# Attention outputs divided by their row sums, causal scores in row tiles, and the probability copies shared evenly by two engines

## The reference

```python
# block 1: heads are mixed in the scores, and the softmax is normalised over the image
# block 2: causal attention; then a quantized FFN
# block 3: causal attention with biases; then a mixture of four experts, two of them active
p = softmax(mask(q @ k.T * HD ** -0.5))     # 256 x 256 a head
o = p @ v
y = o @ w_proj (+ b_proj)
x = x + y
```

## Time and profile before

| | us |
|---|---|
| median of 3 runs | 978.55 |
| lowest and highest | 974.76 and 978.98 |
| profiled execution, whole | 974.61 |
| profiled execution, span | 972.6 |

### The profile page before, as it was taken

How to read it: one execution, slowest core, us unless ns; L and a number is a source line. 1 busy time by engine, 2 the same in 40 slices (tenths; PEclk the granted TensorE clock), 3 DMA queues, 4 the chain that set the end, 5 groups by cost and what they waited for, 6 DMA issues and landing times.

```text
span 972.6 us, 19124 instructions
## 1 busy us (share of the span) xinstructions
PE 808.0 (83%) x5550; PEld 630.5 (65%) x5550; DVE 772.7 (79%) x2166; ACT 632.9 (65%) x1931; POOL 192.6 (20%) x234
## 2 busy tenths in 40 slices
PE   0876698889988755899999486559999997999997
PEld 0762576667766653678887356438778877677775
DVE  7327799999999835699999869938999994688886
ACT  0211587777877513689888564248889874688885
POOL 9001423443234110000000000010000010134344
PEclk9997899999999967799999798779999995799999
DMA  5000000000000091466666200035666650313130
GB/s 184 1 0 1 1 1 0 0 0 0 0 0 0 10 121 28 76 93 97 90 87 83 31 1 1 0 62 83 84 97 96 88 75 0 69 41 82 41 82 17
DMA packets 54355, 44.30 MB, mean 46 GB/s; under 512 B 28592, under 2 KB 42544, under 8 KB 54192
## 3 DMA queue, kind: packets, MB, share of 16 engines
q1 hardware_dynamic: 53872, 42.30, 27.9%
q0 software_dynamic: 448, 1.57, 0.6%
HBM read 12.33 MB, written 3.21 MB: 16 GB/s over the span
## 4 chain that ended last, share of the span: by engine, by line
PE 44%; DVE 12%; DMA 3%; issue 1%; ACT 1%; SPq 1%; POOL 0%; POOLq 0%; DVEq 0%; ACTq 0%
PE ps L839 7%; PE ps L850 6%; PE ps L720 6%; PE ps L624 6%; PE ps L670 5%; PE ps L661 3%; PE ps L626 3%; DVE chst L910 2%; DMA qk<-lo 2%; DVE on L929 2%; PE ps L551 1%; PE ps L634 1%; PE ps L635 1%; PE ps L647 1%; PE ps L826 1%
## 5 line engine op out<-in xcount | busy, mean ns | idle before, releaser
L419 ACT ACTIVATE ee<-ps,nmax 128x128 f32<-128x128 f32 (+1 forms) x588 | 249.5, 443 | 11.7 <-DVE nmax L990 9.9
L1031 DVE TENSOR_SCALAR ee<-ee,rrec 128x128 f32<-128x128 f32 (+1 forms) x588 | 174.8, 360 | 5.2
L720 PE MATMUL ps<-w,ee 128*128 128x128 f32 x960 | 137.0, 279 | 19.9 <-DVE ee L1031 19.9
L406 ACT ACTIVATE big<-ps 128x384 f32<-128x384 f32 (+1 forms) x224 | 113.5, 538 | 40.0 <-PE ps L720 39.4
L720 PEld LDWEIGHTS ps<-w,ee 128*128 128x128 f32 x960 | 103.9, 141 | 45.4 <-DVE ee L1031 35.6
L419 ACT ACTIVATION_READ_ACCUMULATOR ee<-ps,nmax 128x1 f32 x588 | 124.2, 211 | 0.0
L990 DVE TENSOR_REDUCE nmax<-ps 128x2 f32<-128x256 f32 x200 | 101.1, 545 | 18.0 <-PE ps L626 18.0
L624 PE MATMUL ps<-qk 128*128 128x128 f32 (+1 forms) x400 | 103.7, 348 | 13.4 <-DMA qk<-lo 10.8
L296 POOL TENSOR_TENSOR big<-qs,w 96x256 f32<-96x256 f32 x108 | 78.8, 761 | 144.4 <-ACT qs L429 144.4
L1234 DVE TENSOR_TENSOR hhl<-ee,hhl 128x512 fp32r<-128x512 f32 x96 | 81.7, 858 | 27.9 <-ACT hhl L525 26.2
L624 PEld LDWEIGHTS ps<-qk 128*128 128x128 f32 x400 | 79.8, 207 | 31.7 <-issue 17.9
(11 more groups left out here) (224 smaller groups left out, 1365.5 us busy)
## 6 DMA issues: line engine op xcount, KB each, us to landing
qk<-hi SPq DMA_DIRECT2D x36, 192.0 KB, 3.7
qk<-hi SPq DMA_DIRECT2D x72, 96.0 KB, 3.8
qk<-lo SPq DMA_DIRECT2D x36, 192.0 KB, 4.8
qk<-lo SPq DMA_DIRECT2D x72, 96.0 KB, 4.6
big<-moe_gate SPq DMA_DIRECT2D x8, 768.0 KB, 6.9
w<-w_in SPq DMA_DIRECT2D x1, 1831.5 KB, 12.9
xc<-x_in SPq DMA_DIRECT2D x4, 384.0 KB, 5.7
l_mix<-on SPq DMA_DIRECT2D x8, 192.0 KB, 6.6
```

What stands on the lines that cost most here:

```text
L406: nc.scalar.activation(et[:, h, 0:w], ps[:, 4 + hh, 0:w], ACT.Copy).then_inc(own(l, f"et{hh}"), 1)
L419: last = nc.scalar.activation(ee[:, ke, hh, qc, 0:w], src, ACT.Exp, bias=nmax[:, kp, hh, qc:qc + 1], accum_out=rsum[:, kp, hh, qc:qc + 1])
L720: last = nc.tensor.transpose(ps[:, 4 + hh, b * P:(b + 1) * P], ee[:, u, hh, qc, tc * P:(tc + 1) * P], ident)
L1031: last = V.tensor_scalar(v, v, rrec[:, kp, hh, qc:qc + 1], None, ALU.mult)
```

## The change

- The probabilities are not scaled. The values get a column of ones beside each head's 16 (in the half that was zero), so that the weighing yields the row sums too. `normalise_outputs` divides: the unscaled outputs are transposed so that queries lie on partitions (L665 in the new numbering), VectorE takes the reciprocal of the sums (L1043) and multiplies (L1050). In block 1 that takes the place of a copy. In blocks 2 and 3 the result `ob` is transposed back (`outputs_back`, L672), copied by ScalarE to `oc` (L446) and then projected (`project_outputs`, L679); the projection weights are 96 columns in place of 2 x 96.
- In block 1 the sum of squares comes from bn_stats of the unscaled probabilities, four a unit (each 256 columns), and six small instructions after the loop combine them with the squared reciprocals.
- Causal scores are made in row tiles: `qk` holds two heads in 64 rows each, four groups of 16 rows a head. The two heads' products of one query tile follow each other in different halves of the array; the mask is one product per head over both diagonal blocks, after all four. The 16-row groups of the two heads are filled by 12 DMAs an image with half the rows each.
- ScalarE copies three of the six probability tiles an image, VectorE three; before it was four and two.
- The last block's weight split has a buffer of its own and is made earlier, before block 2's attention.

```diff
-STK = 16 * 6
+STK = 16 * 12
...
-        qk = sb("qk", [P, 2, NH, 2, N], F32R)
+        qk = sb("qk", [P, 2, NH // 2, 2, N], F32R)
...
                         for t, a0, a1 in moves:
-                            sp.dma_start(qk[t * HD:(t + 1) * HD, par, :, a0:a1, :].bitcast(F32),
-                                         part[:, a0:a1, :].bitcast(F32)).then_inc(own(l, "stacked"), 16)
+                            for hh in range(2):
+                                r0 = hh * 4 * HD + t * HD
+                                sp.dma_start(qk[r0:r0 + HD, par, :, a0:a1, :].bitcast(F32),
+                                             part[hh * (C // 2):(hh + 1) * (C // 2), a0:a1, :].bitcast(F32)).then_inc(own(l, "stacked"), 16)
...
-                    last = nc.scalar.activation(ee[:, ke, hh, qc, 0:w], src, ACT.Exp, bias=nmax[:, kp, hh, qc:qc + 1],
-                                                    accum_out=rsum[:, kp, hh, qc:qc + 1])
+                        last = nc.scalar.activation(ee[:, ke, hh, qc, 0:w], src, ACT.Exp, bias=nmax[:, kp, hh, qc:qc + 1])
...
+            def outputs_by_channel(l, i):
+
+                act.wait_ge(*upto(l, "oc_ps", i + 2))
+                nc.scalar.activation(oc[0:C, :], ps[0:C, 6, 0:N], ACT.Copy).then_inc(own(l, "oc"), 1)
...
+                            r0 = hh * 4 * HD
+                            mm(ps[:, 2 * kp + hh, qc * N:qc * N + w], qk[r0:r0 + 4 * HD, par, u, 0, qc * P:(qc + 1) * P],
+                               qk[r0:r0 + 4 * HD, par, u, 1, 0:w], start=(qc == 0), stop=False)
+                    for hh in range(2):
+                        diag = ps[:, 2 * kp + hh, :].rearrange("p (b t) -> p b t", t=P)[:, 0::3, :]
+                        last = mm(diag, identb[:, :], mid_dim(maskb[:, :], 1, TPI), start=False, stop=True)
...
+            def outputs_back(l, i):
+
+                pe.wait_ge(*upto(l, "on", i + 2))
+                for q in range(TPI):
+                    last = nc.tensor.transpose(ps[0:C, 6, q * P:(q + 1) * P], ob[:, q, :], ident)
+                last.then_inc(own(l, "oc_ps"), 1)
+
+            def project_outputs(l, i):
+
+                pe.wait_ge(*upto(l, "oc", i + 2))
+                for q in range(TPI):
+                    last = mm(ps[:, 6, q * C:(q + 1) * C], oc[0:ONE + 1, q * P:(q + 1) * P], wa(f"l{l}_p", ONE + 1), start=True, stop=True)
...
+                        if l > 1 and u == 2:
+                            project_outputs(l, i - 1)
                         for hh in range(2):
-                            pe.wait_ge(*upto(l, "norm", 2 * k + (hh + 1)))
+                            pe.wait_ge(*upto(l, "exp", 2 * k + (hh + 1)))
...
                         if u == 0:
                             project_qk(l, i + 2, par)
+                            if l > 1:
+                                outputs(l, i - 1)
                         if u == 1:
-                            outputs(l, i - 1)
+                            if l == 1:
+                                outputs(l, i - 1)
+                            else:
+                                outputs_back(l, i - 1)
...
+            def normalise_outputs(l, i):
+
+                dve.wait_ge(*upto(l, "oq", i + 2))
...
+                V.reciprocal(rec, src[:, :, :, HD]).then_inc(own(l, "orec"), 1)
+                dve.wait_ge(*upto(l, "orec", i + 2))
+                for q in range(TPI):
...
+                    last = V.tensor_tensor(dst.rearrange("p (h d) -> p h d", d=HD), src[:, q, :, 0:HD], last_dim(rec[:, q, :], HD), ALU.mult)
+                last.then_inc(own(l, "on" if l > 1 else "added"), 1)
```

More of the change, by code:

```diff
@@ L652, in outputs @@
                 pe.wait_ge(*upto(l, "ot", i + 2))
-                if l == 1:
+                for q in range(TPI):
                     for g in range(2):
-                        for q in range(TPI):
-                            a = (q * 2 + g) * C
-                            last = nc.tensor.transpose(ps[:, 6, a:a + C], ots[0:C, g, q * P:(q + 1) * P], wb("ident", C)[:, 0:C])
-                else:
-                    for t in range(TPI):
-                        for g in range(2):
-                            last = mm(ps[:, 6, t * C:(t + 1) * C], ots[:, g, t * P:(t + 1) * P], wa(f"l{l}_p")[:, g * C:(g + 1) * C],
-                                      start=(g == 0), stop=(g == 1))
+                        a = (q * 2 + g) * C
+                        last = nc.tensor.transpose(ps[:, 6, a:a + C], ots[0:C, g, q * P:(q + 1) * P], wb("ident", C)[:, 0:C])
+                last.then_inc(own(l, "oq"), 1)
+            def outputs_back(l, i):
[7 more added lines that the diff above has]
+                    last = mm(ps[:, 6, q * C:(q + 1) * C], oc[0:ONE + 1, q * P:(q + 1) * P], wa(f"l{l}_p", ONE + 1), start=True, stop=True)
                 last.then_inc(own(l, "out_ps"), 1)
@@ L1010, in add_outputs @@
             def add_outputs(l, i):
                 dve.wait_ge(*upto(l, "out_ps", i + 2))
-                if l == 1:
-                    for q in range(TPI):
-                        src = ps[:, 6, q * 2 * C:(q + 1) * 2 * C].rearrange("p (h d) -> p h d", d=2 * HD)[:, :, 0:HD]
-                        dst = on1[:, q, i + 1, :] if isinstance(i, int) else on1[:, q, bass.ds(i + 1, 1), :].rearrange("p a c -> p (a c)")
-                        last = V.tensor_copy(dst.rearrange("p (h d) -> p h d", d=HD), src)
-                else:
-                    tv = tok_all[:, bass.ds(i * TPI + TPI, TPI), :]
-                    last = V.tensor_tensor(tv, ps[:, 6, 0:TPI * C].rearrange("p (t c) -> p t c", c=C), tv, ALU.add)
@@ L1021, in add_outputs @@
-                last.then_inc(own(l, "added"), 1)
-            def normalise(l, k, kp, ke):
-                dve.wait_ge(*upto(l, "exp", 2 * k + 2))
-                V.reciprocal(rrec[:, kp, :, :], rsum[:, kp, :, :]).then_inc(own(l, "rec"), 1)
-                dve.wait_ge(*upto(l, "rec", k + 1))
-                for hh in range(2):
-                    for qc in range(TPI):
-                        v = ee[:, ke, hh, qc, 0:scores_cols(l, qc)]
-                        last = V.tensor_scalar(v, v, rrec[:, kp, hh, qc:qc + 1], None, ALU.mult)
-                    last.then_inc(own(l, "norm"), 1)
+                tv = tok_all[:, bass.ds(i * TPI + TPI, TPI), :]
@@ L1034, in _ @@
+                V.tensor_tensor(tv, ps[:, 6, 0:TPI * C].rearrange("p (t c) -> p t c", c=C), tv, ALU.add).then_inc(own(l, "added"), 1)
             for l in (1, 2, 3):
@@ L1058, in _ @@
                         maxima(l, k + 2, j % 2)
-                        if l > 1 and u != 1:
+                        if l > 1 and u == 2:
+                            add_outputs(l, i - 1)
+                        if l > 1:
                             w = len(blocks(l)) * P
-                            dve.wait_ge(*upto(l, "tr", TR0 + 2 * k + 1))
-                            V.tensor_copy(et[:, 2 * u, 0:w], ps[:, 4, 0:w]).then_inc(own(l, "et0"), 1)
+                            for hh in range(1):
+                                dve.wait_ge(*upto(l, "tr", TR0 + 2 * k + hh + 1))
+                                V.tensor_copy(et[:, 2 * u + hh, 0:w], ps[:, 4 + hh, 0:w]).then_inc(own(l, f"et{hh}"), 1)
@@ L1063, in _ @@
                         if l == 1:
-                            dve.wait_ge(sg("l1_norm"), 2 * k + 2)
-                            dve.wait_ge(sg("l1_ssq"), TR0 + k)
-                            for hh in range(1 if u == 2 else 2):
-                                a = ee[:, u, hh, :, :].rearrange("p q t -> p (q t)")
-                                last = V.tensor_tensor_reduce(out=sqj[:, hh, :], in0=a, in1=a, scale=1.0, scalar=0.0, op0=ALU.mult,
-                                                              op1=ALU.add, accum_out=ssq[:, par, 2 * u + hh:2 * u + hh + 1])
@@ L1070, in _ @@
-                            last.then_inc(sg("l1_ssq"), 1)
+                            dve.wait_ge(sg("l1_exp"), 2 * k + 2)
+                            for hh in range(2):
+                                for q in range(TPI):
+                                    last = V.bn_stats(est[:, par, q, 2 * u + hh, :], ee[:, u, hh, q, :])
+                            last.then_inc(sg("l1_est"), 1)
                             if u == 2:
-                                dve.wait_ge(sg("l1_ssq"), TR0 + k + 1)
-                                dve.wait_ge(sg("l1_ssq_act"), i + 1)
-                                V.tensor_copy(ssqa[:, bass.ds(i, 1), :].rearrange("p a h -> p (a h)"), ssq[:, par, :]).then_inc(sg("l1_ssqa"), 1)
```

115 lines of the change are left out of this document (66 added, 49 removed).

## The result

The changed kernel takes **1055.54 us** (median of 4 runs, 1054.69 to 1061.57), the kernel before 978.0 (4 runs, 974.76 to 978.98): a ratio of 1.081, 95% interval 1.077 to 1.086. It is slower by 8%; the forecast was 1042.

The account below looks back on a forecast made before the run. The causal loops were taken as bound by the longer of the DMA cycle, 11.2 us, and TensorE's turn, 10.5. 75 + 8 + 7 - 26 + 2 = +66 on 974.6 gave 1041, forecast 1042 us; band 1030 to 1050, range 1003 to 1068.

Parts of the forecast that it names:

- Block 1's loop, -26: First block's attention loop: without scaling, transposes wait for the exponentials alone; 1.62 us less an image, 26 us for 16.
- VectorE's cover: First block's loop: VectorE finishes reciprocal and products about 1 us before TensorE's weighing; without that, at most 5 us return.
- Behind block 1, +2: After the first block's loop: about six linked VectorE instructions, at most 0.33 us each, precede the variance; +2 us.
- The stack DMAs, 11.2: Causal loops: six more issues add 3.7 us, a shorter landing returns 1.1; the DMA cycle grows from 8.62 to 11.2 us.
- TensorE's own turn, 8.9, with the wait 10.5: Causal loops: TensorE's work 8.9 us an image, no gain from row tiles; waiting 1.6 for normalised outputs makes 10.5.
- The loops, +75: Both causal loops: +2.5 us an image over 15 periods in each of two layers, +75 us.
- Ahead of and behind the loops, +8 and +7: Around the causal loops: two stacks in series ahead, +8 in all; five hand-overs and the new wait behind, +3.5 each.
- dear tiles: Rival, causal loops: score unit 1.2 us, TensorE's turn 11.4 to 11.9, or idle time lowers the clock; +87, 1062; chance 0.14.
- Cheap issues: Rival, causal loops: a 48-row issue costs about half, so TensorE's turn of 10.5 us holds; +40, 1015 us; chance 0.22.
- Faster: Rival, causal loops: VectorE has outputs ready, TensorE never late at the transposes back; period 8.0, -38, 937 us; chance 0.06.
- the wait for `on`: Causal loops, u=1: TensorE waits 1.6 us for normalised outputs before transposing back; loss and gain cancel at period 9.3.
- The signs named beforehand: Right: block 1's image -1.6, bursts 11 us apart, `ob` wait 1.5 or more. Wrong: issues near 0.3, unit below 0.7, clock below 1.

Follow-up runs that it names:

- one move on VectorE: Changed kernel with VectorE's reciprocal and two output products put ahead of the middle head pair's maxima in blocks 2 and 3: 998.38 us, ratio 1.021.
- the run that filled the wait: Changed kernel with three more unused q-projection products an image on TensorE, ahead of the transposes back in blocks 2 and 3: 1022.57 us, ratio 1.046.
- the repaired whole change: Changed kernel with its output path half a head pair earlier on three engines and three of twelve stacking transfers issued by GpSimd: 985.42 us, ratio 1.008.
- the kernels with GpSimd's transfers: Three of twelve stacking transfers issued by GpSimd: kernel before plus row tiles 980.62 us, also with block 1's change 962.28, changed kernel with earlier output path 985.42.
- the row tiles alone: Kernel before with only the row-tiled scores and twelve stacking transfers in blocks 2 and 3, old sums and scaling kept: 1010.02 us, ratio 1.033.

## Why the prediction was right, and where not

- **Block 1's loop, -26.** Right: an image takes 11.81 us instead of 13.50, 1.69 less where I had 1.62, which is 27 in 16 images, and the one wait was gone. VectorE's cover held, and bn_stats took 0.35 us each (192 of them in 67.0 us of busy time) in the place of 0.33.
- **Behind block 1, +2.** Too small: it was 27 - 23.1 = +3.9 up to the product of the sums of squares. VectorE's linked instructions took from 301.37 to 304.47, 3.1 us, since some have 384 elements and take 0.7; TensorE waited 4.00 us for them, where it had waited 0.71. A consequence that I didn't have at all came behind it: the clock is 0.50 from 305 to 325, and the 32 products that took 3.74 us take 7.03. That is 3.3 of the +4.5 up to block 2.
- **The stack DMAs, 11.2.** The issues were right (0.63 against 0.62). The term that failed is the landing: I took 3.5, the least of the trace of before, for the last transfer of half the bytes; it was 2.08. The cycle is 9.7 to 9.9, **below** TensorE's turn. So the step that named what bounds the changed loop ("the longer of 11.2 and 10.5 holds") was wrong, and two kernels show it: half the transfers gave 6 us, and one move on VectorE gave 57.
- **TensorE's own turn, 8.9, with the wait 10.5.** The sum came out, 10.6, made of 8.46 of work, 1.83 and 0.30 of waiting; but the work was 0.4 too long and the waits 0.5 too short, and that these cancel is luck. The wait was 1.83 for 1.6, and the mechanism as described: the maxima, the copy, the reciprocal and the products in a row, 2.06 us. The small second wait, 0.30 for the add, was one that I had called covered. The row tiles came out at a gain of 0.34 a turn where I took none. The row that grows ahead of a row-tiled unit agrees with the Trainium skill, TensorEngine Tiling (Array Packing), Key Properties. Its Theoretical Speedup of up to 2x isn't reached: the unit of two heads goes from 0.89 to 0.66, a factor of 1.35. The masking products are in it; the four score products alone, each counted to the next start, go from 0.70 to 0.43 (473.39 to 473.82), a factor of 1.6.
- **The loops, +75.** 86 measured, by another cause than the forecast's. What held was the second limit, 1.9 us x 30 = 57, and with it a clause that I had put in a rival, that idle time lowers the granted clock: 29 by the difference, 27 by the run that filled the wait. The wrong 11.2 stood by chance near the 11.4 and 11.7 that the clock makes of 10.6, so that the total came near is luck in its largest term.
- **Ahead of and behind the loops, +8 and +7.** 4.1 and 8.3. The step from the profiled execution to the median has a slip: 0.4% on 1041 is 1045, not 1042.
- **The rivals.** The measured 1055.5 lies outside the forecast's own band of 1030 to 1050, in that of "dear tiles", which had a chance of 0.14. "Cheap issues" had the right limit for a wrong reason, and without the clock it would have been near: the kernel with the filled wait, whose turn is TensorE's, took 1023. "Dear tiles or the clock" had the clock right and the tiles wrong. "Faster" failed where the text said that it would be decided, at the wait for `on`.
- **The signs named beforehand.** Two of those for "right" came: block 1's image and the wait for `ob`. The third didn't: the bursts are 10.59 apart, not 11, and in the loop no DMA releases the key split. Two of those for "wrong" came as well, a score unit below 0.7 (0.66) and a granted clock below 1.

What stays open: why turns with a low clock come in groups, mostly three or four in a row between undisturbed ones, what limits the repaired whole change at 9.18 us, and where the 7 us at the end of the kernels with GpSimd's transfers come from.

## What to carry to other kernels

Work that leaves one engine can cost more than it gives when a new hand-over comes with it. The division put behind a reduction made TensorE wait for VectorE in the middle of its turn; its place in VectorE's queue was worth 57 us here. No run shows a gain in the causal loops from the load taken off VectorE and ScalarE: with the transfers split alike, the turn is 9.18 with the late division and 8.47 with the old sums. When a wait and a queue have cycles within 1 us of each other, compute both with their landings and don't name the winner by a difference smaller than the spread of the landing. Measure the parts of a combined change apart: block 1's part alone is 2% faster than before, and it was inside a change that is 8% slower. An issue placed on a compute engine's queue is paid by what is queued behind it, so take the engine that waits, and measure the whole program, since here the cost lay at the loop's head and at the program's end.

## What the runs showed of the hardware

- **Idle TensorE can cost twice.** With 1.83 and 0.30 us of idle time in each turn of 10.6 the granted clock fell to 1.2 GHz in stretches, 27 us in two loops; with 1.5 us of useless products in the wait it stayed at 2.4 GHz, and the kernel was 33 us faster for doing more. One wait of 1.51 in a turn of 9.68 (the row tiles alone) left the clock at 1.00. The Trainium skill, TensorE: Matmul & The Clock Gate, Part 1: The HAM clock gate, ties the clock to how busy TensorE has recently been; these runs agree.
- **A transfer of half the rows lands earlier.** The lines of the profile on transfers, median us from issue to landing last, of the changed kernel and then of the kernel before:

```profile
qk<-hi SPq DMA_DIRECT2D x72, 96.0 KB, 2.8
qk<-hi SPq DMA_DIRECT2D x144, 48.0 KB, 2.1
```
```profile
qk<-hi SPq DMA_DIRECT2D x36, 192.0 KB, 3.7
qk<-hi SPq DMA_DIRECT2D x72, 96.0 KB, 3.8
```

  96 KB from 48 rows took 2.8 us and from 96 rows 3.8, so it isn't the bytes that decide. The kernel with the row tiles undone has the old values again, 3.7 and 3.8. An issue on SyncE's queue costs the same for all, some 0.6 us.
- **The same three issues** take 1.9 us of SyncE's queue, 2.11 of ScalarE's and 1.6 to 1.7 of GpSimd's. On ScalarE they made the loop longer and on GpSimd shorter, but the kernels with them on GpSimd ran 9.4 us past the issue of the last store, all others 2.4 to 2.5.
